# A state-space layer on one core: sums by accumulating transposes, some inputs from ScalarE, gate and gated result on POOL

## The reference

```
a = layernorm(x); xn = layernorm(a)
u, res = split(xn @ W_in + b_in)        # 2 x 256 channels
u = silu(causal_conv4(u)); dt, Bm, Cm = split(u @ W_x)     # 64, 16, 16
delta = softplus(dt @ W_dt + b_dt); A = -exp(A_log)        # A: 256 x 16
for t:  h = exp(delta_t * A) * h + (delta_t * u_t) * B_t   # h: 256 channels x 16 states
        y_t = sum over states n of h[:, n] * C_t[n]
y = (y + u * D) * silu(res)
x = x + a + y @ W_out + b_out
```

## Time and profile before

| | |
|---|---|
| three runs | 2678.16, 2684.52, 2678.65 us; median 2678.65 |
| the profiled execution | 2678.22 us, span 2676.4 us |
| busy over the span | PE 79%, DVE 65%, ACT 50%, POOL 47% |
| granted TensorE clock, mean | 0.87 of full |
| 1740 to 2345 us, about this layer | PE 547.27, DVE 529.68, ACT 383.62, POOL 473.12 us busy of 605; clock 0.97 |

### The profile page before, as it was taken

One profiled execution on the slowest core, in us unless ns is written; L12 is line 12 of the kernel. 1 busy time (PEld: TensorE's weight loads), 2 busy tenths in 40 slices (PEclk: granted clock), 3 DMA queues, 4 the chain that ended last, 5 costly groups with the idle time before them and its releaser, 6 DMA issues. The chain is left out here.

```text
span 2676.4 us, 47828 instructions
## 1 busy us (share of the span) xinstructions
PE 2116.4 (79%) x15968; PEld 1477.6 (55%) x15968; DVE 1734.4 (65%) x4210; ACT 1330.9 (50%) x2849; POOL 1264.3 (47%) x1313
## 2 busy tenths in 40 slices
PE   5999999999896881493799987689999999842870
PEld 2666666666684671372455546555556555531650
DVE  5777777777567563013677756579988889846113
ACT  4665756566342471132355555466666667420223
POOL 5654546464210006354321205487778777700662
PEclk8999999999995685697799998889999999955885
DMA  8200000000110001122333330000000000010113
GB/s 250 69 2 2 1 2 2 2 2 1 37 36 0 1 0 44 52 76 83 95 87 79 94 96 0 0 1 1 0 0 0 0 0 0 0 32 6 44 43 96
DMA packets 104252, 89.45 MB, mean 33 GB/s; under 512 B 12076, under 2 KB 91206, under 8 KB 104006
## 3 DMA queue, kind: packets, MB, share of 16 engines
q1 hardware_dynamic: 96934, 72.67, 9.8%
q0 software_dynamic: 7168, 14.73, 1.7%
HBM read 59.02 MB, written 40.96 MB: 37 GB/s over the span
## 5 line engine op out<-in xcount | busy, mean ns | idle before, releaser
L3344 POOL TENSOR_SCALAR mb_w<-mb_duT,mb_bT 128x256 f32<-128x256 f32 x512 | 468.0, 933 | 116.5 <-PE bank L3354 85.1
L3279 DVE TENSOR_TENSOR_SCAN mb_hs<-mb_dA,bank 128x512 f32<-128x512 f32 x256 | 300.8, 1205 | 34.5 <-issue 23.9
L3373 PE MATMUL bank<-mb_hc,ident 128*128 128x512 f32 x512 | 256.2, 624 | 15.7 <-DVE mb_hc L3289 15.4
L38 POOL TENSOR_TENSOR scrap<-ones 128x1 f32<-128x1 f32 x64 | 12.5, 195 | 469.2 <-DVE gla_ss L414 261.4
L3335 ACT ACTIVATE mb_dA<-mb_delta,mb_A 128x255 f32<-128x255 f32 x512 | 216.4, 495 | 7.3 <-DVE mb_hs L3279 7.1
L2083 ACT ACTIVATE e_hid<-bank,e_b 128x512 f32<-128x512 f32 (+1 forms) x128 | 79.6, 634 | 258.4 <-PE bank L2127 186.2
L2501 DVE TENSOR_REDUCE ra_mx<-bank 128x2 f32<-128x512 f32 x256 | 163.9, 686 | 59.2 <-PE bank L2355 56.5
L2591 ACT ACTIVATE ra_pT<-bank 128x512 f32<-128x512 f32 x256 | 141.1, 600 | 112.5 <-PE bank L2377 112.2
L3354 PE MATMUL bank<-ident,mb_w 128*128 128x128 f32 x1024 | 149.9, 280 | 34.3 <-DVE mb_hs L3279 26.2
L565 DVE TENSOR_TENSOR gla_mid<-bank,gla_ex 128x512 f32<-128x512 f32 x128 | 88.4, 690 | 120.8 <-ACT gla_ex L551 120.6
L581 DVE COPY_PREDICATED gla_sT<-c_seen,bank 128x768 f32<-128x768 int32 x128 | 131.0, 1024 | 41.3 <-issue 41.3
(11 more groups left out here) (536 smaller groups left out, 5657.8 us busy)
## 6 DMA issues: line engine op xcount, KB each, us to landing
results<-const_empty SPq DMA_DIRECT2D x2, 4096.0 KB
e_got<-results SPq DMA_DIRECT2D x32, 256.0 KB, 3.2
rope_rows<-ra_part SPq DMA_DIRECT2D x48, 128.0 KB, 1.9
ra_k<-rope_rows SPq DMA_DIRECT2D x32, 192.0 KB, 3.3
ra_q<-rope_rows SPq DMA_DIRECT2D x32, 192.0 KB, 4.2
queue<-const_spare_rows SPq DMA_DIRECT2D x1, 4128.0 KB
e_x<-queue SPq DMA_DIRECT2D x8, 516.0 KB
e_w<-in_L_ffn_w SPq DMA_DIRECT2D x2, 2048.0 KB, 8.2
```

What stands on the lines that cost most here:

```text
L3279: dve.tensor_tensor_scan(hs[n // 2 % 2][:, n % 2, :, :].rearrange("p c t -> p (c t)"), dA[n % RD][:, :, :].rearrange("p c t -> p (c t)"), ...
L3344: ins = pool.tensor_scalar(w[n % RH][:, h, :], duT[k][:, h, :], bT[k][:, h, n:n + 1], None, ALU.mult)
L3373: ins = pe.matmul(YB[:, :], g.ident[:, :], hc[grp % 2][:, j, :, :].rearrange("p c t -> p (c t)"), start=(n == 0), stop=(n == NS - 1))
```

## The change

The sum over the states is turned round: `pe_sum` transposes each 128x128 block of the products and accumulates the transposes in PSUM, so that `YB` holds the sum with time on the partitions; `act_result` copies it to `yT` on ACT; `pe_channels` transposes it back, into the bank `RB`, where `dve_finish` reads it. The inputs `w` of states 3, 7, 11 and 15 are written by ACT (`act_inputs`), with its own semaphore. The gate is computed on POOL in two operations (`pool_gate`, at state 4 of its own sequence), and the product with the gate too (`pool_finish`, at state 7 of the next). The result `yy` and `yT` lie in the free tile `g.xT`, one of each, so `uc` no longer waits for the output matmuls and `dve_finish` waits for those of the sequence before. Stage 9 on PE moves from state 9 to 10, the turn back stands at 2, `dve_finish` at 4, `pe_out` at 7, and the residual with the statistics two states later.

```diff
--- before.py
+++ after.py
@@ -3083,7 +3083,8 @@
     dA = [sb(f"dA{k}", [P, ND, SEQ]) for k in range(RD)]
     hs = [sb(f"hs{k}", [P, 2, ND, SEQ]) for k in R]
     hc = [sb(f"hc{k}", [P, 2, ND, SEQ]) for k in R]
-    yy = uc
+    yy = g.xT[:, 2 * DI:4 * DI].rearrange("p (c t) -> p c t", c=ND)
+    yT = g.xT[:, 0:2 * DI].rearrange("p (h d) -> p h d", h=2)
     prep, a_ready, bin_psum = sig("prep"), sig("aready"), sig("binp")
     win_ready, taps_ready, cum_ready, bin_ready = sig("win"), sig("taps"), sig("cum"), sig("bin")
     conv_ready = sig("conv")
@@ -3091,12 +3092,12 @@
     rs12_ready, scales_ready = sig("nrs12"), sig("nscales")
     names = ["xn", "xTp", "xT", "urp", "ub", "rc", "rp", "r", "er", "gr", "uc", "xdp", "xd", "dp", "rest", "mid", "bTp", "bT", "bc", "z", "az",
              "ez", "lz", "dl", "du", "duTp", "duT", "dA", "w", "dbu", "cp", "hs", "hc", "y", "yy", "op", "x0", "x",
-             "st", "mv", "mvs"]
+             "st", "mv", "mvs", "yT", "yb", "wa", "yg", "gp"]
     (xn_ready, xT_psum, xT_ready, ur_psum, ub_ready, rc_ready, r_psum, r_ready, er_ready,
      gr_ready, uc_ready, xd_psum, xd_ready, d_psum,
      rest_ready, mid_ready, bT_psum, bT_ready, bc_ready, z_ready, az_ready, ez_ready, lz_ready, dl_ready, du_ready, duT_psum, duT_ready,
      dA_ready, w_ready, dbu_psum, bc_psum, hs_ready, hc_ready, y_psum, yy_ready, o_psum, x0_ready, x_ready,
-     st_ready, mv_ready, mvs_ready) = [sig(n) for n in names]
+     st_ready, mv_ready, mvs_ready, yT_ready, yb_psum, wa_ready, yg_ready, gp_ready) = [sig(n) for n in names]
     DB, RC, YB = g.pb[0:2], g.pb[2:4], g.pb[4]
     TB, UB, RB = g.pb[5], g.pb[6], g.pb[7]
 
@@ -3139,8 +3140,6 @@
     def dve_prepare(dve, s, k, stage):
         if stage == 4:
             dve.wait_ge(rc_ready, s + 1)
-            if not (isinstance(s, int) and s < 2):
-                dve.wait_ge(o_psum, s - 1)
             dve.scalar_tensor_tensor(out=uc[k][:, :, :], in0=e1[:, :, :], scalar=1.0, in1=cv[:, :, :],
                                      op0=ALU.add, op1=ALU.mult).then_inc(uc_ready, 1)
         if stage == 5:
@@ -3290,20 +3289,14 @@
                           RC[grp % 2][:, :].rearrange("p (n t) -> p n t", n=2).unsqueeze(2)
                           .broadcast_to([P, 2, ND, SEQ]), ALU.mult).then_inc(hc_ready, 1)
 
-    def dve_gate(dve, s, k):
-        dve.wait_ge(er_ready, s + 1)
-        dve.scalar_tensor_tensor(out=gr[k][:, :, :], in0=e2[:, :, :], scalar=1.0, in1=rs[:, :, :],
-                                 op0=ALU.add, op1=ALU.mult).then_inc(gr_ready, 1)
-
     def dve_finish(dve, s, k):
-        dve.wait_ge(y_psum, s * (NS // 2) + NS // 2)
+        dve.wait_ge(yb_psum, s + 1)
+        if not first(s):
+            dve.wait_ge(o_psum, s)
         for c in range(ND):
-            ins = dve.scalar_tensor_tensor(out=yy[k][:, c, :], in0=uc[k][:, c, :], scalar=g.m_D[:, c:c + 1],
-                                           in1=YB[:, c * 256:(c + 1) * 256], op0=ALU.mult, op1=ALU.add)
+            ins = dve.scalar_tensor_tensor(out=yy[:, c, :], in0=uc[k][:, c, :], scalar=g.m_D[:, c:c + 1],
+                                           in1=RB[:, c * 256:(c + 1) * 256], op0=ALU.mult, op1=ALU.add)
         ins.then_inc(yy_ready, 1)
-        dve.wait_ge(yy_ready, s * 2 + 1)
-        dve.wait_ge(gr_ready, s + 1)
-        dve.tensor_tensor(yy[k][:, :, :], yy[k][:, :, :], gr[k][:, :, :], ALU.mult).then_inc(yy_ready, 1)
 
     def dve_residual(dve, s):
         dve.wait_ge(o_psum, s + 1)
@@ -3335,6 +3328,11 @@
             ins = act.activation(dA[n % RD][:, c, 1:SEQ], delta[k][:, c, 1:SEQ], ACT.Exp, scale=A[:, c, n:n + 1])
         ins.then_inc(dA_ready, 1)
 
+    def by_act(n):
+        return n % RH == RH - 1
+
+    PER_POOL, PER_ACT = NS - NS // RH, NS // RH
+
     def pool_inputs(pool, s, k, n):
         if n == 0:
             pool.wait_ge(duT_ready, s + 1)
@@ -3344,9 +3342,34 @@
             ins = pool.tensor_scalar(w[n % RH][:, h, :], duT[k][:, h, :], bT[k][:, h, n:n + 1], None, ALU.mult)
         ins.then_inc(w_ready, 1)
 
+    def act_inputs(act, s, k, n):
+        act.wait_ge(duT_ready, s + 1)
+        if n >= RH or not first(s):
+            act.wait_ge(dbu_psum, s * NS + (n - RH + 1))
+        for h in range(2):
+            ins = act.activation(w[n % RH][:, h, :], duT[k][:, h, :], ACT.Copy, scale=bT[k][:, h, n:n + 1])
+        ins.then_inc(wa_ready, 1)
+
+    def pool_gate(pool, s, k):
+
+        pool.wait_ge(er_ready, s + 1)
+        if s >= 2:
+            pool.wait_ge(yg_ready, s - 1)
+        pool.tensor_tensor(gr[k][:, :, :], e2[:, :, :], rs[:, :, :], ALU.mult).then_inc(gp_ready, 1)
+        pool.wait_ge(gp_ready, s + 1)
+        pool.tensor_tensor(gr[k][:, :, :], gr[k][:, :, :], rs[:, :, :], ALU.add).then_inc(gr_ready, 1)
+
+    def pool_finish(pool, s, k):
+        pool.wait_ge(yy_ready, s + 1)
+        pool.wait_ge(gr_ready, s + 1)
+        pool.tensor_tensor(yy[:, :, :], yy[:, :, :], gr[k][:, :, :], ALU.mult).then_inc(yg_ready, 1)
+
     def pe_inputs(pe, s, n):
 
-        pe.wait_ge(w_ready, s * NS + (n + 1))
+        if by_act(n):
+            pe.wait_ge(wa_ready, s * PER_ACT + (n // RH + 1))
+        else:
+            pe.wait_ge(w_ready, s * PER_POOL + (n - n // RH + 1))
         if n >= 2 or not first(s):
             pe.wait_ge(hs_ready, s * NS + (n - 1))
         for c in range(ND):
@@ -3367,29 +3390,46 @@
     def pe_sum(pe, s, grp):
         pe.wait_ge(hc_ready, s * (NS // 2) + (grp + 1))
         if grp == 0 and not first(s):
-            pe.wait_ge(yy_ready, s * 2 - 1)
+            pe.wait_ge(yT_ready, s)
         for j in range(2):
             n = 2 * grp + j
-            ins = pe.matmul(YB[:, :], g.ident[:, :], hc[grp % 2][:, j, :, :].rearrange("p c t -> p (c t)"),
-                            start=(n == 0), stop=(n == NS - 1))
+            for h in range(2):
+                for c in range(ND):
+                    at = h * DI + c * P
+                    ins = pe.matmul(YB[:, at:at + P], hc[grp % 2][:, j, c, h * P:(h + 1) * P], g.ident[:, :],
+                                    start=(n == 0 and at == 0), stop=(n == NS - 1 and at == 3 * P), is_transpose=True)
         ins.then_inc(y_psum, 1)
 
-    def pe_out(pe, s, k):
-        pe.wait_ge(yy_ready, s * 2 + 2)
+    def pe_channels(pe, s):
+
+        pe.wait_ge(yT_ready, s + 1)
         if not (isinstance(s, int) and s == NSEQ - 1):
             pe.wait_ge(r_ready, s + 2)
+        for c in range(ND):
+            for h in range(2):
+                ins = pe.transpose(RB[:, c * SEQ + h * P:c * SEQ + (h + 1) * P], yT[:, h, c * P:(c + 1) * P], g.ident[:, :])
+        ins.then_inc(yb_psum, 1)
+
+    def act_result(act, s):
+        act.wait_ge(y_psum, s * (NS // 2) + NS // 2)
+        if not first(s):
+            act.wait_ge(yb_psum, s)
+        act.activation(yT[:, :, :], YB[:, :].rearrange("p (h d) -> p h d", h=2), ACT.Copy).then_inc(yT_ready, 1)
+
+    def pe_out(pe, s, k):
+        pe.wait_ge(yg_ready, s + 1)
         for h in range(2):
             o = RB[:, h * P:(h + 1) * P]
             for c in range(ND):
-                pe.matmul(o, yy[k][:, c, h * P:(h + 1) * P], g.W_out[:, c, :], start=(c == 0), stop=False)
+                pe.matmul(o, yy[:, c, h * P:(h + 1) * P], g.W_out[:, c, :], start=(c == 0), stop=False)
             ins = pe.matmul(o, g.ones[0:1, :], g.b_out[:, :], start=False, stop=True)
         ins.then_inc(o_psum, 1)
 
     AHEAD = 4
     DVE_WHEN = {6: (4,), 8: (5,), 9: (7,), 10: (6,)}
     ACT_WHEN = {1: (0,), 3: (1, 2), 7: (4,), 8: (5,), 9: (6,), 11: (8, 9)}
-    PE_WHEN = {0: (0,), 1: (1,), 2: (2,), 6: (4,), 7: (5,), 8: (7,), 9: (9,), 11: (6,)}
-    IN_PLACE, FINISH, OUT, RESIDUAL, GATE = 0, 2, 4, 7, 7
+    PE_WHEN = {0: (0,), 1: (1,), 2: (2,), 6: (4,), 7: (5,), 8: (7,), 10: (9,), 11: (6,)}
+    IN_PLACE, BACK, FINISH, POOL_GATE, POOL_FINISH, OUT, RESIDUAL = 0, 2, 4, 4, 7, 7, 9
 
     def turns(start, body, end):
 
@@ -3417,8 +3457,6 @@
                 dve_read(dve, s, n // 2 - 1)
             elif n == 0 and not first(s):
                 dve_read(dve, s - 1, NS // 2 - 1)
-            if n == GATE and nxt is not None:
-                dve_gate(dve, s, k)
             if not first(s):
                 if n == RESIDUAL:
                     dve_residual(dve, s - 1)
@@ -3434,7 +3472,6 @@
 
     def dve_end(dve):
         dve_read(dve, NSEQ - 1, NS // 2 - 1)
-        dve_gate(dve, NSEQ - 1, 1)
         dve_finish(dve, NSEQ - 1, 1)
         dve_residual(dve, NSEQ - 1)
         dve_stats(dve, NSEQ - 1)
@@ -3448,6 +3485,7 @@
             act_prepare(act, 0, 0, stage)
         for n in range(AHEAD):
             act_decay(act, 0, 0, n)
+        act_inputs(act, 0, 0, RH - 1)
         act.wait_ge(scales_ready, 2)
 
     def act_body(act, s, k, nxt):
@@ -3460,11 +3498,18 @@
                 act_decay(act, nxt, 1 - k, n + AHEAD - NS)
             if n == IN_PLACE and not first(s):
                 act_residual(act, s - 1)
+            if n == 1 and not first(s):
```

(18 more changed lines are left out.)

## The result

The changed kernel takes 2641.09 us (median of 4 runs, 2640.11 to 2643.68) beside 2678.4 us of the kernel before on the same chip: ratio 0.9861, 95% interval 0.984 to 0.9882. Forecast were 2620 us and a range of 2598 to 2652. It is faster, inside the range, and by 37 us instead of 58.

The account below looks back on a forecast made before the run. VectorE was taken to set the 37.19 us period, with TensorE making it wait. Work 31.7 plus waits 1.7 gives 33.4 us; 15 periods save 57 us, the end about 1, total 58: 2620 us, range 2598 to 2652.

Parts of the forecast that it names:

- The work: Busy time per period after the change: VectorE 31.7 us, TensorE about 29, ScalarE 28.4, POOL 25.8.
- The two operations off VectorE: Gate (0.75 us) and final product (0.99, median 0.91) leave VectorE: 1.7 us less per sequence, nothing replacing them.
- VectorE sets the period: VectorE, busy 33.3 to 34.0 us of each 37.19 us period, is the bound, and TensorE makes it wait.
- The sums: On TensorE, sums by transposes: 6.3 us less, net -5.7 with the turn back; queues before scan inputs 0.8 us shorter.
- `uc` loses its wait: VectorE's 0.9 us wait before `uc` for the output matmuls goes, the result no longer lying in its buffer.
- I keep 0.7 of 1.2 us: VectorE's wait before `delta` for ScalarE's logarithm: 0.7 us of today's 1.2 us was forecast to remain.
- priced at "nothing": Output matmuls at state 7 wait for POOL's product, some 4 us ahead of them: no cost claimed.
- Rival (a): ScalarE becomes the pace, half its waiting staying: period 34.9 us, kernel 2644 us; chance 0.17 (up to 2660).
- Rival (c): TensorE falls to half clock for more of the layer and takes the lead: 2709 us; chance 0.10.
- Rival (d): Result and gate on POOL slow four VectorE operations by 0.2 us each: 12 us, 2632 us; forecast with it 0.60.
- the argument from `mb_bc`: VectorE's `mb_bc`, two SBUF operands, took 0.449 us, no more than `mb_rest`, so this trace showed no holding by POOL.
- the strict rule: VectorE operations with two SBUF inputs and GpSimd ones exclude each other entirely: some 0.4 us each, 24 us, 2644 us.

Follow-up runs that it names:

- e3: The changed kernel with the gate (state 7) and the final product back on VectorE; period 34.63 us, ratio 0.9851 to the kernel before.
- e10: e9 with the gate and final product back on VectorE, as in e3; period 34.20 us, ratio 0.985 to the kernel before.
- e4: The changed kernel with the sums by identity matmuls as before, without copy and turn back; period 36.52 us, ratio 0.9935 to the kernel before.
- e11: The changed kernel with gate and product on VectorE and all 16 inputs on POOL; period 35.14 us, ratio 0.99 to the kernel before.
- e2: The changed kernel with POOL writing all 16 inputs `w`, none by ScalarE; period 37.2 us, ratio 1.0014 to the kernel before.
- e8: The kernel before with only the result `yy` in two buffers of its own; period 36.77 or 37.6 us, ratio 0.9987.
- e1: The changed kernel with the projection to delta ahead of the output matmuls on TensorE at state 7; period 33.96 us, ratio 0.9808 to the kernel before.
- e5: The changed kernel with ScalarE's softplus ahead of the decay at state 9, copy of B behind the logarithm; period 34.29 us, ratio 0.9836.
- e7: e6 with both halves of TensorE's convolution one state later, read by ScalarE at state 4; period 33.65 us, ratio 0.9813 to the kernel before.
- e6: The changed kernel with the orders of e1 and e5 and the residual at state 10; period 33.51 us, ratio 0.9804 to the kernel before.
- e9: e6 with the output matmuls on TensorE at state 8 instead of 7; period 33.30 us, ratio 0.9777 to the kernel before.
- e12: e9 with ScalarE's in-place scaling of x at state 3 instead of 0; period 33.16 us, ratio 0.9778 to the kernel before.

## Why the prediction was right, and where it was off

- **The work** was right on all four engines, to 1 us or better, and so were its rows: sums 1.09 us, ScalarE's inputs 0.496 us each, POOL's 128x512 operations 1.28 (forecast 1.05, 0.42 and 1.27).
- **The two operations off VectorE** were counted in full, 1.7 us; its busy time fell by 1.4 (33.1 to 31.7). e3 shows 0.23 us of them in the changed kernel, e10 0.90 where waits had been cleared. The mechanism "VectorE sets the period" was too simple.
- **The sums** were credited only with fewer waits. They carry most of the change: 2.1 of the 2.4 us between periods at full clock (e4), and with only the own buffer and the new places beside them they still give 1.6 (e11, 35.14 for 36.77). The parts do not add up: undoing the quarter alone costs 2.8 (e2), since POOL then holds the layer.
- **The number** is in the range partly by luck: the ledger of work and waits closes (31.7 + 2.6 = 34.4), but what each part was credited with in it isn't what taking it away costs.
- **The own buffer**: "`uc` loses its wait" was right, and worth nothing on the kernel before (e8).
- **The step that failed** is "I keep 0.7 of 1.2 us" for the wait before `delta`, measured at 1.65. Two things were wrong in it. "VectorE's own way to it gets the residual and statistics in place of the gate": residual and first statistics stood behind `uc` before the change too (states 7 and 8) and still do (9 and 10), while the gate left, and the rest of the statistics now comes behind `delta`; from the end of `uc` to the end of the statistics VectorE takes 8.3 us (1870.73 to 1879.06) for 9.2 before. And the output matmuls at state 7 were priced at "nothing" for POOL's product alone; nobody asked what is queued behind them on TensorE. It is the projection to delta, 0.9 us late; e1, which puts it first, begins the softplus 0.98 us sooner. The chain to the logarithm became 0.4 us shorter instead of 0.8 (9.94 us from the end of `uc` for 10.34).
- **Why 1 us too little came**, beyond that step: the sum took each remaining wait as a time that can be removed. e1, e5, e7 and e8 each removed one and got 0.44, 0.11, a loss beside e6, and 0. These runs fit a ring, delta, softplus, `duT` and `xT` on ScalarE, convolution, inputs, `uc`, delta, with ways through VectorE, TensorE and ScalarE that are equal to some tenths of a microsecond. The forecasts made by it came within 0.3 us for the period of e9, 0.2 for the loss in e10 and 0.1 for the gain in e12. e7, made before it was put so, missed by 1.0.
- **Rival (a)** came nearest in its number (2644), but not by its mechanism; it gave the right hint, the `xT` copy. As the pace by itself ScalarE is excluded by e12, in the order of e9 (0.87 us less work in its unbroken stretch, 0.14 us won); in the changed kernel e5 shows it as one of several nearly equal ways.
- **Rival (c)** did not come. The clock falls at the hand-over as often as before, in 7 of the 14 periods after the first (mean 0.95 in such a period, 1.00 in the others; 0.96 over the layer), but a fall costs 0 to 0.7 us of a period where it cost 0.8 to 0.9. In most of the variants' traces it falls in none to three periods, so this count isn't a property of the change.
- **Rival (d)** was put too low by the argument from `mb_bc`. It was not VectorE but POOL that paid there: its second `w` in this row of the kernel before takes 1.20 us, where one takes 0.93 as a rule.

```profile
2031.61 2.10 POOL L3344 TENSOR_SCALAR mb_w<-mb_duT,mb_bT 128x256 f32<-128x256 f32 x2
...
2032.55 0.45 DVE L3152 SCALAR_TENSOR_TENSOR mb_bc<-mb_mid,c_part_signs,mb_rest 128x256 bf16<-128x256 bf16 x1
```

  The three new POOL operations do no harm in the changed kernel (`uc` 0.683 us, `delta` and delta*u 0.69), so the 12 us, or 24 by the strict rule, did not come. But the interaction is real, and taking a product off VectorE took it out of POOL's way: see below.
- That the quarter is needed at all (e2, 2.8 us per period) was in the prediction only as POOL's total; the bound is that total and the wait for `duT`.

e9 and e12 beat both kernels: 2621.06 and 2620.78 us, 0.9777 and 0.9778 of the kernel before. Open is which of the waits left there (0.25 to 0.44 us each, 1.5 us in all in e9) could still be won; e7 says that the convolution's place is not the whole answer. Not tried are the sums by transposes at the old places in the order, and the changed kernel without the own buffer.

## What to carry to other kernels

When engines hand to one another in a ring, the sum "busy time of the busiest engine, with the removed waits struck out" is only a lower bound: an edit that shortens one way gains no more than its distance to the next longest way round, and the removed wait comes up again at the next hand-over. When a step is moved in an in-order queue, ask what stands behind it at the new place, also where the step itself is early enough. A trace in which one wait has vanished and the period has not moved is the sign of such a ring; then remove two or three waits together (e6, e9), and read the total.

## What the runs showed of the hardware

**The clock rises over transposes alone.** In the changed kernel at one hand-over the granted clock fell to 0.50, 1.2 of 2.4 GHz, after a stretch in which TensorE was busy for 0.97 us and had waited 2.43 us. In the next it did nothing but transposes, all 18 of its records, and was then granted 1.00 again. Stages, and the matmuls that begin in the middle one:

```profile
2086.80:2090.20 3.40, 0.97 (x7) 0.57 (x6) 2.97 (x7) 3.37 (x7) 0.00 (x0) 1.00 0.00 0
2090.20:2093.60 3.40, 3.40 (x18) 3.07 (x17) 3.40 (x5) 2.87 (x7) 1.44 (x2) 0.50 0.00 0
2093.60:2097.00 3.40, 2.95 (x25) 2.38 (x24) 3.40 (x4) 3.40 (x10) 3.40 (x5) 1.00 0.00 0
```

```profile
2090.37 1.06 PE L3269 MATMUL bank<-ident,mb_z 128*128 128x128 f32 x4
2091.23 1.06 PE L3377 MATMUL bank<-ident,mb_w 128*128 128x128 f32 x4
2092.18 1.77 PE L3399 MATMUL bank<-ident,mb_hc 128*128 128x128 f32 x8
```

The Trainium skill ("TensorE: Matmul & The Clock Gate", Part 4) says that transposes don't bring the full clock. For 32-bit transposes these rows show the opposite, and a period in which some 140 of 200 matmul records are transposes ran at 1.00 (the first of the two stages shown with the result); the falls are single stretches at the hand-over.

**VectorE and POOL hold each other up on SBUF, and either can be the one that pays.** A VectorE operation with two SBUF inputs takes 1.04 us instead of 0.69 beside POOL's `w` (e11). The other way round, a POOL write of 128x256 that begins 0.06 us behind `uc` takes 1.42 us instead of 0.93, the largest value in

```profile
L3342 POOL TENSOR_SCALAR mb_w<-mb_duT,mb_bT x384: 914/926/1417, 1750.4 to 2289.6; 128x256 f32<-128x256 f32 x192
```

Which one pays isn't simply the one whose record starts second: in the kernel before, at 2164.56 us, the final product took 1.08 us although the `w` beside it, of the usual 0.92, is recorded as starting 0.07 us later.

The Trainium skill ("SBUF — State Buffer", two separate sides) says that such a pair exclude each other for whole instructions. That they get in each other's way the runs bear out, in both directions. The whole instruction they don't: the product of e11 at 1899.86 ends 0.09 us behind the `w` that began with it, though it takes 0.69 us alone. The loss measured at one meeting is at most 0.4 us for VectorE and 0.55 for POOL.

It also explains the 0.91 us of the product in the earlier trace rows, which starts 0.11 us into a `w` of POOL, and why POOL's load matters to VectorE where POOL is not late: by e11 against e3, 0.5 us of each period.
